# The product stage's first five h tiles: loaded by the up stage into the room of the up weights

## The chip, the cores and the metric

The kernel runs on one core of one Trainium2 chip. The metric is the device time of one execution in microseconds (us). The engines named here are PE (TensorE, matmuls), DVE (VectorE), ACT (ScalarE), POOL (GpSimd) and SP (SyncE, which in these stages issues every DMA).

## What is computed

The reference is a decoder layer on 4 sequences of 1024 tokens of width 512: self-attention with a norm, cross-attention with a norm, and a gated feed-forward of inner width 1536 in which the tensors are quantised and dequantised between the steps. The change concerns the feed-forward alone:

```python
def act_qdq(x):
    qmax = 2.0 ** (ACT_BITS - 1) - 1.0
    scale = jnp.maximum(jnp.max(jnp.abs(x)) / qmax, 1e-12)
    return jnp.clip(jnp.round(x / scale), -qmax - 1.0, qmax) * scale
...
x = act_qdq(x)
up = act_qdq(x @ lpbq_dequant(w_up).T)
gate = act_qdq(x @ lpbq_dequant(w_gate).T)
sig = fixed_qdq_u16(jax.nn.sigmoid(gate))
gate = act_qdq(gate * sig)
o = act_qdq(gate * up)
return o @ lpbq_dequant(w_down).T
```

Each `act_qdq` needs the largest magnitude of a whole tensor before its first element can be quantised. So the stages of the feed-forward can't flow into one another: each ends with a maximum, and the next begins with a scale.

## The kernel before, in words

All tensors of the feed-forward are feature-major: a tile has 128 features in the partitions and tokens along the free dimension. There are T = 4096 tokens, 8 groups of 512 tokens, and 12 feature tiles f of 128 features. Features 0 to 5 (RES = 6) of the up product stay in SBUF (`rows`, called `res` in the functions); features 6 to 11 ("spilled") are written to the HBM tensor `scr_up` (`y_dram`).

**The up stage** (`up_phase`, L1806) takes 96 steps n, of 512 tokens and one feature tile each. In a step PE makes twelve matmuls with the up weights `wu_hi` and `wu_lo`; SP loads a gate tile (`load_gate`, L1852), ACT, POOL and DVE make h = gate * sigmoid(gate) of it in a ring of seven buffers `v_w`, and SP stores it to the HBM tensor `scr_h` (`store_h`, L1858); for the spilled features SP stores an up tile too (L1872). SP's instructions are one queue in written order: behind step 95's up store stand `store_h(NT - 1)`, the store of the last h tile, and then waits until every store has landed:

```python
                store_h(NT - 1)
                for j in range(NY):
                    sp.wait_ge(y_out[j], 16 * sum(1 for m in range(NG * (FT - RES)) if m % NY == j))
                for j in range(NW):
                    sp.wait_ge(h_out[j], 16 * sum(1 for n in range(NT) if n % NW == j))
```

The block of the stage (L1839) ends in a barrier of all engines. Then the stage's semaphores are cleared (L59), and a second barrier follows (L60); `Kit.clear` does both, once for each kit that has semaphores.

**The quantisers** (`quantisers`, "quh") turn the two maxima into scales, with a few small instructions of DVE and PE and barriers of their own.

**The product stage** (`product_phase`, L1975) takes 48 tiles of 128 x 1024 in f32 (512 KB), features in the order 0, 6, 1, 7, 2, 8 and so on, four token blocks of each; so four tiles whose up part is in `rows` alternate with four spilled ones. Per tile ACT quantises h (L2045) and up (L2049), DVE multiplies (L2064) and takes the maximum of the tile before (L2057). SP loads h from `scr_h` into a ring of six buffers `j_h` (L2019), for spilled tiles also up from `scr_up` into `j_u` (L2024), and stores a spilled tile's result to `scr_o` (L2036). The load of tile n waits for the product of tile n - 6, and step n of SP's loop issues load n + 5 ahead of the store of tile n, which waits for product n. Before the loop SP issues the loads of tiles 0 to 4.

Then `product_quantiser` and `down_phase` follow; the latter is the second large matmul stage and ends the kernel.

Of the kernel before, what the change touches and what calls it, by code (L numbers as in the profile page):

```python
# [49 lines left out]
class Kit:  # L50


    def __init__(self, nc, ctx):
        self.nc, self.ctx, self.sems = nc, ctx, []
        ctx.callback(self.clear)
# [1747 lines left out]
                dve.wait_ge(scaled, 2)  # L1803


def up_phase(nc, x_dram, scale, wts, gate_dram, sg, isg, hunit, y_dram, res, h_dram, ymax, hmax):  # L1806

# [2 lines left out]
    with ExitStack() as ctx:  # L1812
# [26 lines left out]
        with nc.Block() as block:  # L1839

            @block.sync
            def _(sp):
                def load_x(g):
                    for j, dst in enumerate((xh, xl)):
                        sp.dma_start(dst[g % 2][:], x_dram[j][g]).then_inc(x_in[g % 2], 16)

                def load_gate(n):
                    g, o = divmod(n, FT)
                    if n >= NW:
                        sp.wait_ge(hmaxed, n - NW + 1)  # L1850
                        sp.wait_ge(h_out[n % NW], 16 * (n // NW))
                    sp.dma_start(wk[n % NW][:], gate_dram[o, :, g * GT:(g + 1) * GT]).then_inc(g_in[n % NW], 16)  # L1852

                def store_h(n):
                    g, o = divmod(n, FT)
                    sp.wait_ge(prod, n + 1)
                    sp.sem_inc(stood, 1)
                    sp.dma_start(h_dram[o, :, g * GT:(g + 1) * GT], wk[n % NW][:]).then_inc(h_out[n % NW], 16)  # L1858

                load_x(0)  # L1860
                for n in range(NW - LATE):
                    load_gate(n)
                load_x(1)
                for n in range(NT):
                    g, o = divmod(n, FT)
                    if n + NW - LATE < NT:
                        load_gate(n + NW - LATE)
                    if n > 0:
                        store_h(n - 1)
                    if o >= RES:  # L1870
                        sp.wait_ge(evicted, n + 1)
                        sp.dma_start(y_dram[o, :, g * GT:(g + 1) * GT], y[spilled(n) % NY][:]).then_inc(y_out[spilled(n) % NY], 16)  # L1872
                    if o == FT - 1 and g + 2 < NG:
                        sp.wait_ge(summed, n + 1)
                        load_x(g + 2)
                store_h(NT - 1)
                for j in range(NY):
                    sp.wait_ge(y_out[j], 16 * sum(1 for m in range(NG * (FT - RES)) if m % NY == j))
                for j in range(NW):
                    sp.wait_ge(h_out[j], 16 * sum(1 for n in range(NT) if n % NW == j))  # L1880
# [91 lines left out]
                dve.wait_ge(done, 2)  # L1972


def product_phase(nc, h_dram, y_dram, res, ish, isu, o_dram, omax):  # L1975

    W, NH, NU, NO = 1024, 6, 4, 4
    TR = T // W  # L1980
    rows, spare = list(range(RES)), list(range(RES, FT))
    order = []
    while rows or spare:
        order += [rows.pop(0)] if rows else []
        order += [spare.pop(0)] if spare else []
    tiles = [(f, j) for f in order for j in range(TR)]
    NT = len(tiles)
    with ExitStack() as ctx:
        kit = Kit(nc, ctx)
        h = [kit.sb(f"j_h{j}", [P, W], F32) for j in range(NH)]  # L1990
        u = [kit.sb(f"j_u{j}", [P, W], F32) for j in range(NU)]
        o = [kit.sb(f"j_o{j}", [P, W], F32) for j in range(NO)]
        magic = kit.sb("j_magic", [P, 1], F32)
        tmax = kit.sb("j_tmax", [P, NT], F32)
        h_in, u_in, stored = ([kit.sem(f"j_{n}{j}") for j in range(k)] for n, k in (("h_in", NH), ("u_in", NU), ("out", NO)))
        ready, added, prod, maxed, done, stood = (kit.sem(f"j_{n}") for n in ("ready", "added", "prod", "maxed", "done", "stood"))

        def spilled(n):
# [13 lines left out]
        with nc.Block() as block:  # L2012
            @block.sync
            def _(sp):
                def load(n):
                    f, j = tiles[n]
                    if n >= NH:
                        sp.wait_ge(prod, n - NH + 1)
                    sp.dma_start(h[n % NH][:], h_dram[f, :, j * W:(j + 1) * W]).then_inc(h_in[n % NH], 16)  # L2019
                    m = spilled(n)  # L2020
                    if m is not None:
                        if m >= NU:
                            sp.wait_ge(prod, tile_of(m - NU) + 1)
                        sp.dma_start(u[m % NU][:], y_dram[f, :, j * W:(j + 1) * W]).then_inc(u_in[m % NU], 16)  # L2024
# [201 lines left out]
def feed_forward(nc, c, res, moments, x1_dram, w_dram, scratch, out):  # L2226
# [4 lines left out]
    with ExitStack() as ctx:  # L2231
# [8 lines left out]
        with ExitStack() as up_scope:  # L2240
            wu = [Kit(nc, up_scope).sb(f"wu_{n}", [P, FT, KT, P], F16) for n in ("hi", "lo")]
            with ExitStack() as gate_scope:
# [7 lines left out]
                quantisers(nc, c, "qx", [of("x")])  # L2250
                gate_phase(nc, c, x2, res[:, T // P * D:], x2_dram, scale["x"], inverse["x"], wg, gate_dram, x_dram, pmax["gate"], tiles(wu, 1) + down_tiles)
            quantisers(nc, c, "qg", [of("gate")])
            up_phase(nc, x_dram, scale["x"], wu, gate_dram, scale["gate"], inverse["gate"], hunit, up_dram, res, h_dram,
                     pmax["up"], pmax["h"])
        quantisers(nc, c, "quh", [of("up"), of("h", hunit)])
        product_phase(nc, h_dram, up_dram, res, inverse["h"], inverse["up"], o_dram, pmax["o"])
        product_quantiser(nc, c, pmax["o"], scale["h"], scale["up"], scale["o"], inverse["o"])
        down_phase(nc, o_dram, res, scale["o"], inverse["o"], wd, x2_dram, out)

# [52 lines left out]
```

## Time and profile before

| what | value |
|---|---|
| time, median of 3 runs | 3060.09 us (3058.86 to 3063.71) |
| the profiled execution, its own time | 3056.02 us |
| its span in the trace | 3054.2 us |
| PE busy, share of the span | 86% |
| DVE, ACT, POOL busy | 74%, 61%, 59% |
| up stage | from 2390 us to 2652 us of the span |
| product stage | from 2656.7 us to 2781.8 us |
| down stage | from 2785 us to the end |

Positions in the trace are microseconds from the start of the span. A DMA has two times: SP issues it, which takes some 0.3 to 0.5 us of SP's queue, and it lands later; the landing raises the semaphore that others wait for. Rates in GB/s are what the 16 DMA engines moved together.

### The profile page before, as it was taken

How to read it: one execution, taken by the hardware profiler on the slowest of the kernel's cores; microseconds unless marked ns; L12 is line 12 of the kernel's file. 1: busy time of each engine (PE TensorE's matmuls, PEld its weight loads, DVE VectorE, ACT ScalarE, POOL GpSimd, SP SyncE). 2: the span in 40 equal slices, each digit the busy share in tenths (PEclk: the TensorE clock that was granted, in tenths of full speed). 3: DMA queues.
4: the chain of work that ended last, by engine and by line, in shares of the span. 5: the costliest groups of instructions: out<-in, count | busy, mean ns of one | idle time of the engine just before them, and what ended most of it. 6: DMA issues, size and time to landing. Idle time of an engine off the chain costs nothing. (4 is left out here: it accounts for less than half of the span.)

```text
span 3054.2 us, 77257 instructions
## 1 busy us (share of the span) xinstructions
PE 2622.1 (86%) x24103; PEld 1414.8 (46%) x24103; DVE 2263.1 (74%) x4431; ACT 1872.6 (61%) x3765; POOL 1815.2 (59%) x1209
## 2 busy tenths in 40 slices
PE   7999688888886969999999999993999899603999
PEld 4555345555554534555555555551444344201444
DVE  8888767777775777888888888865333477697776
ACT  3444377777775536777777777774333577695333
POOL 3444489999997317999999999994000244300000
PEclk9999889999998989999999999996999999856999
DMA  8999634434445661223233242235443688796332
GB/s 305 334 334 329 220 101 127 137 126 136 133 133 171 234 231 48 54 83 88 78 114 90 78 122 83 82 88 188 167 165 151 219 278 287 267 417 252 127 112 82
DMA packets 331176, 517.02 MB, mean 169 GB/s; under 512 B 41057, under 2 KB 162785, under 8 KB 331058
## 3 DMA queue, kind: packets, MB, share of 16 engines
q1 hardware_dynamic: 327586, 508.88, 50.1%
q0 software_dynamic: 1952, 6.29, 0.7%
q8 instruction: 55, 0.90, 0.1%
q10 hardware_dynamic: 1520, 0.43, 0.1%
q14 instruction: 63, 0.52, 0.0%
HBM read 266.10 MB, written 194.28 MB: 151 GB/s over the span
## 5 line engine op out<-in xcount | busy, mean ns | idle before, releaser
L1301 POOL TENSOR_TENSOR cross_plo<-cross_p 128x2048 f16<-128x2048 f32 (+1 forms) x256 | 856.7, 3376 | 46.1 <-ACT cross_p L1082 46.1
L1196 DVE CUSTOM_DVE_ANT_0 cross_junk<-cross_sc,rows 128x1024 bf16<-128x1024 f32 x512 | 617.9, 1222 | 109.1 <-PE cross_sc L946 101.4
L1082 ACT ACTIVATE cross_p<-cross_st 128x512 f32<-128x512 f32 x1024 | 556.1, 595 | 210.2 <-PE cross_st L993 210.1
L1301 POOL TENSOR_TENSOR self_plo<-self_p 128x1024 f16<-128x1024 f32 (+7 forms) x512 | 576.8, 1160 | 15.2 <-ACT self_p L1082 14.7
L1082 ACT ACTIVATE self_p<-self_st,self_strip 128x512 f32<-128x512 f32 (+3 forms) x768 | 414.7, 582 | 141.0 <-PE self_st L991 110.8
L1196 DVE CUSTOM_DVE_ANT_0 self_junk<-self_sc,self_strip 128x1024 bf16<-128x1024 f32 (+7 forms) x512 | 371.1, 753 | 133.4 <-PE self_sc L952 132.4
L988 PE MATMUL cross_st<-cross_qa,cross_ka 97*128 97x512 f16 x1024 | 395.7, 386 | 2.6 <-DMA cross_qa<-cross_mrow 1.2
L993 PE MATMUL cross_st<-rows,idbig 128*128 128x512 f16 x1024 | 391.3, 382 | 0.0
L1017 PEld LDWEIGHTS cross_o<-cross_vh,cross_p 128*128 128x128 bf16 x4096 | 270.9, 97 | 78.1 <-issue 24.5
L1017 PE MATMUL cross_o<-cross_vh,cross_p 128*128 128x65 f16 x4096 | 298.1, 191 | 7.0 <-POOL cross_plo L1301 6.8
L1928 POOL TENSOR_SCALAR v_w<-v_w 128x512 f32<-128x512 f32 x96 | 59.8, 623 | 400.1 <-ACT v_w L1905 400.0
L1018 PE MATMUL cross_o<-cross_vh,cross_plo 128*128 128x33 f16 x4096 | 291.7, 179 | 0.0
L988 PE MATMUL self_st<-self_qa,self_ka 98*128 98x512 f16 (+3 forms) x768 | 244.1, 333 | 50.8 <-ACT self_p L1082 46.0
L1018 PEld LDWEIGHTS cross_o<-cross_vh,cross_plo 128*128 128x128 f16 x4096 | 250.0, 96 | 53.4
L952 PE MATMUL self_sc<-self_ka,self_qa 96*128 96x512 f16 (+3 forms) x768 | 213.0, 334 | 33.7 <-DMA self_ka<-scr_k_hi 18.7
L1017 PE MATMUL self_o<-self_vh,self_p 128*128 128x65 f16 x2304 | 199.3, 192 | 40.1 <-DVE self_osum L1219 19.8
L130 PE MATMUL gt_acc<-rows,wg_hi 128*128 128x512 f16 x768 | 229.9, 381 | 1.5 <-DVE rows L124 1.5
L945 PE MATMUL cross_sc<-cross_ka,cross_qa 32*128 32x512 f16 x512 | 200.4, 392 | 21.2 <-DMA cross_kx<-scr_k_hi 12.3
L946 PE MATMUL cross_sc<-cross_kx,cross_qa 32*128 32x512 f16 x512 | 200.4, 392 | 0.0
L1017 PEld LDWEIGHTS self_o<-self_vh,self_p 128*128 128x128 bf16 x2304 | 163.2, 98 | 74.3 <-issue 43.1
L1018 PE MATMUL self_o<-self_vh,self_plo 128*128 128x33 f16 x2304 | 192.0, 179 | 0.0
L988 PEld LDWEIGHTS cross_st<-cross_qa,cross_ka 97*128 97x128 f16 x1024 | 99.7, 97 | 188.4 <-ACT cross_p L1082 94.8
(266 smaller groups left out, 5859.0 us busy)
## 6 DMA issues: line engine op xcount, KB each, us to landing
self_strip<-self_strips SPq DMA_DIRECT2D x64, 516.0 KB, 3.2
scr_gate<-gt_y SPq DMA_DIRECT2D x96, 256.0 KB, 2.1
v_w<-scr_gate SPq DMA_DIRECT2D x96, 256.0 KB, 4.0
scr_h<-v_w SPq DMA_DIRECT2D x96, 256.0 KB, 4.1
j_h<-scr_h SPq DMA_DIRECT2D x48, 512.0 KB, 9.5
d_o<-scr_o SPq DMA_DIRECT2D x9, 1536.0 KB
scr_up<-v_y SPq DMA_DIRECT2D x48, 256.0 KB, 4.2
j_u<-scr_up SPq DMA_DIRECT2D x24, 512.0 KB, 12.2
```

Source lines behind the costliest of these rows:

```text
L130: mm = nc.tensor.matmul(out, a, b, start=(n == 0), stop=(n == len(terms) - 1))
L945: nc.tensor.matmul(sc[slot % 2][:, 0:GT], qa[j][0:HD, qt * P:(qt + 1) * P], ka[j][0:HD, 0:GT], start=True, stop=True)
L946: nc.tensor.matmul(sc[slot % 2][:, GT:S], qa[j][HD:2 * HD, qt * P:(qt + 1) * P], kx[j][HD:2 * HD, :], start=True, stop=True).then_inc(scor ...
L952: mm = nc.tensor.matmul(sc[slot % 2][:, k - k0:k - k0 + w], qa[j][0:3 * HD, qt * P:(qt + 1) * P], ka[j][0:3 * HD, k:k + w], start=True, st ...
L988: mm = nc.tensor.matmul(out[:, 0:w], lhs, qa[j][0:KR, q0:q1], start=True, stop=causal)
L993: mm = nc.tensor.matmul(out[:, 0:w], c["idbig"][:], nm[kt][:, q0:q1], start=False, stop=True)
L1017: nc.tensor.matmul(out[:, qt % 4, :], high[:, q], vh[n % NQK][:, kt, :], start=first, stop=False, skip_group_check=True)
L1018: mm = nc.tensor.matmul(out[:, qt % 4, 0:HD + 1], rest[:, q], vh[n % NQK][:, kt, 0:HD + 1], start=False, stop=last_kt, skip_group_check=True)
L1082: nc.scalar.activation(p32[j][:, b + q0 - a:b + q1 - a], stp[cc % 2][:, 0:q1 - q0], ACT.Exp, bias=bias, scale=SM).then_inc(expd, 1)
L1196: nc.vector.tensor_tensor_reduce(junk[slot % 2][:, 0:w], sc[slot % 2][:, 0:w], bias, 1.0, -3e38, ALU.add, ALU.max, qmax[n % 2][:, qt:qt + ...
L1301: nc.gpsimd.tensor_tensor(plo[j][:, a:z], p32[j][:, a:z], high, ALU.subtract).then_inc(lo_g, 1)
L1928: nc.gpsimd.tensor_scalar(wk[n % NW][:], wk[n % NW][:], 65536.0, MAGIC, ALU.mult, ALU.add).then_inc(inc, 1)
```

## The change

The product stage's six h buffers are no longer tiles of their own: they become views into the up weights `wu_hi` and `wu_lo`, whose last reader is the last matmul of the up stage. A class `EarlyProducts` holds these views, their six semaphores and the first five tiles of the product's order, which are (feature, token block) = (0, 0), (0, 1), (0, 2), (0, 3) and (6, 0).

- In the up stage SP, after the up store of step 95 and before `store_h(NT - 1)`, waits for the last matmul (`summed` at NT), then for the stores of `scr_h` that the five tiles read, and issues the five loads.
- In the product stage SP issues no h load for tiles 0 to 4; the up load of tile 4 stays.
- The room of the up weights and the new semaphores live until the end of the product stage: the quantisers and the product stage move inside `up_scope`. When that scope ends, the kit of `EarlyProducts` clears its semaphores, with one more barrier of all engines, between the product stage and `product_quantiser`.

```diff
@@ up_phase, sync
                     if o == FT - 1 and g + 2 < NG:
                         sp.wait_ge(summed, n + 1)
                         load_x(g + 2)
+                sp.wait_ge(summed, NT)
+                for k, (f, j) in enumerate(following.tiles):
+                    n = ((j + 1) * (PW // GT) - 1) * FT + f
+                    sp.wait_ge(h_out[n % NW], 16 * (n // NW + 1))
+                    following.load(sp, k)
                 store_h(NT - 1)
@@ new
+PW, PH = 1024, 6
+class EarlyProducts:
+    def __init__(self, kit, wu, h_dram):
+        whole = [w[:].rearrange("p t k n -> p (t k n)").bitcast(F32) for w in wu]
+        each = FT * KT * P // 2 // PW
+        self.h = [whole[j // each][:, j % each * PW:(j % each + 1) * PW] for j in range(PH)]
+        self.h_in = [kit.sem(f"j_h_in{j}") for j in range(PH)]
+        self.h_dram, self.tiles = h_dram, product_order()[:PH - 1]
+
+    def load(self, sp, n):
+        f, j = self.tiles[n]
+        sp.dma_start(self.h[n], self.h_dram[f, :, j * PW:(j + 1) * PW]).then_inc(self.h_in[n], 16)
@@ product_phase
-        h = [kit.sb(f"j_h{j}", [P, W], F32) for j in range(NH)]
+        h, h_in = given.h, given.h_in
@@ product_phase, sync, load(n)
                     if n >= NH:
                         sp.wait_ge(prod, n - NH + 1)
-                    sp.dma_start(h[n % NH][:], h_dram[f, :, j * W:(j + 1) * W]).then_inc(h_in[n % NH], 16)
+                    if n >= NH - 1:
+                        sp.dma_start(h[n % NH][:], h_dram[f, :, j * W:(j + 1) * W]).then_inc(h_in[n % NH], 16)
@@ feed_forward
             quantisers(nc, c, "qg", [of("gate")])
+            given = EarlyProducts(Kit(nc, up_scope), wu, h_dram)
             up_phase(nc, x_dram, scale["x"], wu, gate_dram, scale["gate"], inverse["gate"], hunit, up_dram, res, h_dram,
-                     pmax["up"], pmax["h"])
-        quantisers(nc, c, "quh", [of("up"), of("h", hunit)])
-        product_phase(nc, h_dram, up_dram, res, inverse["h"], inverse["up"], o_dram, pmax["o"])
+                     pmax["up"], pmax["h"], given)
+            quantisers(nc, c, "quh", [of("up"), of("h", hunit)])
+            product_phase(nc, given, h_dram, up_dram, res, inverse["h"], inverse["up"], o_dram, pmax["o"])
         product_quantiser(nc, c, pmax["o"], scale["h"], scale["up"], scale["o"], inverse["o"])
```

## Rows read from the trace of the kernel before

**Rows 1.** Page: span; chain that ended last, by engine.

```profile
span 3054.2 us, 77257 instructions
PE 8%; DVE 0%; DMA 0%; ACT 0%; issue 0%; DVEq 0%; ACTq 0%
```

**Rows 2.** Windows by stage: length, each engine's busy time, clock, DMA share, GB/s.

```profile
2390.00:2651.90 261.90, 250.90 (x1152) 113.13 (x1152) 181.17 (x290) 193.78 (x289) 115.18 (x192) 0.98 0.83 273
2651.90:2656.70 4.80, 0.69 (x2) 0.32 (x2) 2.01 (x10) 0.00 (x0) 0.00 (x0) 0.50 0.00 0
2660.00:2776.00 116.00, 0.00 (x0) 0.00 (x0) 105.50 (x92) 110.35 (x95) 0.00 (x0) 0.50 1.03 416
```

**Rows 3.** Timeline, ACT, in the product stage: start, duration, idle before.

```profile
2709.45 1.24 ACT L2045 ACTIVATE j_h<-j_h,j_magic,inverse_h 128x1024 f32<-128x1024 f32 x1 [1.01 <-DMA j_h<-scr_h]
...
2769.79 1.24 ACT L2045 ACTIVATE j_h<-j_h,j_magic,inverse_h 128x1024 f32<-128x1024 f32 x1 [1.01 <-DMA j_h<-scr_h]
```

**Rows 4.** Lines, product stage: busy, mean ns of one.

```profile
L2045 ACT ACTIVATE j_h<-j_h,j_magic,inverse_h 128x1024 f32<-128x1024 f32 x48 | 59.1, 1231 | 19.1 <-DMA j_h<-scr_h 18.7
```

**Rows 5.** DMA view, product stage: packets, MB, share of 16 engines.

```profile
q1 hardware_dynamic: 13824, 50.34, 100.4%
```

**Rows 6.** Timeline, DVE, ACT and PE at the boundary of the two stages.

```profile
2644.99 0.38 PE L130 MATMUL v_acc<-v_xh,wu_lo 128*128 128x512 f16 x1
2650.69 0.23 DVE L1971 TENSOR_REDUCE pmax_h<-v_htmax 128x1 f32<-128x96 f32 x1
2652.75 0.23 DVE L1672 COPY quh_wide<-pmax_up 128x128 f32<-128x128 f32 x1 [1.83 <-PEq L60]
2656.78 0.06 DVE L2053 MEMSET j_magic<- 128x1 f32 x1 [1.34 <-PEq L60]
2660.75 1.24 ACT L2045 ACTIVATE j_h<-j_h,j_magic,inverse_h 128x1024 f32<-128x1024 f32 x1 [14.65 <-DMA j_h<-scr_h]
```

**Rows 7.** Timeline, SP's queue: start and duration of each DMA issue.

```profile
2648.09 0.42 SPq L1872 DMA_DIRECT2D scr_up<-v_y  x1
2649.51 0.32 SPq L1858 DMA_DIRECT2D scr_h<-v_w  x1
2656.70 2.34 SPq L2019 DMA_DIRECT2D j_h<-scr_h  x5
...
2664.40 0.32 SPq L2019 DMA_DIRECT2D j_h<-scr_h  x1
```

**Rows 8.** Waits of SP's queue, 2645 to 2662: us in total, times, longest.

```profile
SPq L1880 <- DMA scr_h<-v_w: 1.5, 1, 1.5
```

**Rows 9.** DMA issues, one each, tiles 0, 1, 2, 3, last h store: us to landing.

```profile
j_h<-scr_h SPq DMA_DIRECT2D x1, 512.0 KB, 4.0
...
j_h<-scr_h SPq DMA_DIRECT2D x1, 512.0 KB, 5.0
...
j_h<-scr_h SPq DMA_DIRECT2D x1, 512.0 KB, 5.8
...
j_h<-scr_h SPq DMA_DIRECT2D x1, 512.0 KB, 6.6
...
scr_h<-v_w SPq DMA_DIRECT2D x1, 256.0 KB, 2.0
```

**Rows 10.** DMA issues at 2556.6 to 2558, a gate tile behind two x loads.

```profile
v_xh<-scr_xq_hi SPq DMA_DIRECT2D x1, 512.0 KB, 6.4
...
v_w<-scr_gate SPq DMA_DIRECT2D x1, 256.0 KB, 7.8
```

**Rows 11.** Page, DMA issues of the gate tiles: median us to landing.

```profile
v_w<-scr_gate SPq DMA_DIRECT2D x96, 256.0 KB, 4.0
```

**Rows 12.** Line L2036, the product's stores: landing, shortest, median, longest.

```profile
DMA to landing us min/median/max: 2.6/8.7/9.9
```

**Rows 13.** Lines L1839 and L60 at 2652: barrier, clear, barrier.

```profile
L1839 DVEq EVENT_SEMAPHORE  x1: 21/21/21, 2652.0 to 2652.0; - x1
...
L60 DVEq EVENT_SEMAPHORE  x1: 21/21/21, 2652.6 to 2652.6; - x1
```

More of the change, by code:

```diff
@@ L1803, in _, with up_phase @@
                 dve.wait_ge(scaled, 2)
-def up_phase(nc, x_dram, scale, wts, gate_dram, sg, isg, hunit, y_dram, res, h_dram, ymax, hmax):
+def up_phase(nc, x_dram, scale, wts, gate_dram, sg, isg, hunit, y_dram, res, h_dram, ymax, hmax, following):
     NT, NR, NY, NW, LATE = NG * FT, 4, 3, 7, 3
@@ L1972, in _, with product_order @@
                 dve.wait_ge(done, 2)
-def product_phase(nc, h_dram, y_dram, res, ish, isu, o_dram, omax):
-    W, NH, NU, NO = 1024, 6, 4, 4
-    TR = T // W
+PW, PH = 1024, 6
+def product_order():
     rows, spare = list(range(RES)), list(range(RES, FT))
@@ L1985, in product_phase @@
         order += [spare.pop(0)] if spare else []
-    tiles = [(f, j) for f in order for j in range(TR)]
+    return [(f, j) for f in order for j in range(T // PW)]
+class EarlyProducts:
[8 more added lines that the diff above has]
+        sp.dma_start(self.h[n], self.h_dram[f, :, j * PW:(j + 1) * PW]).then_inc(self.h_in[n], 16)
+def product_phase(nc, given, h_dram, y_dram, res, ish, isu, o_dram, omax):
+    W, NH, NU, NO = PW, PH, 4, 4
+    TR = T // W
+    tiles = product_order()
     NT = len(tiles)
@@ L1994, in product_phase @@
         tmax = kit.sb("j_tmax", [P, NT], F32)
-        h_in, u_in, stored = ([kit.sem(f"j_{n}{j}") for j in range(k)] for n, k in (("h_in", NH), ("u_in", NU), ("out", NO)))
+        u_in, stored = ([kit.sem(f"j_{n}{j}") for j in range(k)] for n, k in (("u_in", NU), ("out", NO)))
         ready, added, prod, maxed, done, stood = (kit.sem(f"j_{n}") for n in ("ready", "added", "prod", "maxed", "done", "stood"))
```

## The prediction

> **What bounds the kernel now.** I read the page first. The chain that ended last names only 8% of the span [rows 1], all in the down stage, because it can't be followed back over the barriers that part the stages. So the change has to be judged from its own stretch, stage by stage: whatever moves the end of the product stage moves everything behind it by as much, and nothing before step 95 of the up stage is touched.
>
> The windows by stage come next [rows 2]. In the up stage PE is busy for 250.9 of 261.9 us. Between the stages, from 2651.9 to 2656.7, DMA moves nothing. In the product stage, from 2660 to 2776, DMA's share is 1.03 and it moves 416 GB/s without a break, while ACT has 110.35 us of work in 116. So DMA looks like the bound there. The timeline of ACT agrees: from tile 21 on it stands still for 1.01 us at every eighth tile until an h tile has landed, the first time before 2709.45 and the fourth before 2769.79, so 20.11 us apart [rows 3]. Up to the first stop it took 2709.45 - 1.01 - 2660.75 = 47.7 us for 21 tiles [rows 3, 6], 2.27 us each; eight tiles at that pace are 18.2 us; eight tiles of transfers are 8 h loads, 4 up loads and 4 stores of 512 KB, 8.39 MB, and at 416 GB/s these are 20.2 us. The stage as a whole moves 50.34 MB [rows 5], 96 transfers of 1.26 us. What is worth something in this stage is DMA work taken out of it, not a shorter wait of an engine.
>
> Then the boundary [rows 6, 7, 8]. PE's last matmul starts at 2644.99, DVE's last maximum at 2650.69. SP issues the last h store at 2649.51, and it lands 2.0 us later [rows 9], at 2651.5; SP is held for 1.5 us until then [rows 8], and it is the last to reach the barrier. The quantisers start at 2652.75, and the product stage's SP issues its first load at S = 2656.70, 5.2 us after that landing. ACT starts at 2660.75, 4.05 us after S, with tile 0.
>
> **The change, step by step.** *(a) The five loads in the up stage.* SP is through with the up store at 2648.51 [rows 7]. PE is long done, and the `scr_h` tiles that the five loads read were stored long before (the latest is step 84, eleven steps of 261.9 / 96 = 2.7 us back [rows 2]), so none of the new waits costs more than its own execution, some 0.03 us (a semaphore instruction of DVE is 21 ns [rows 13]). From 2648.55 SP issues five loads; the same five take 2.34 us in the product stage [rows 7]. With six waits SP arrives at the last h store at about 2651.06 instead of 2649.51, 1.55 us late by issue alone.
>
> The larger cost is what that store finds ahead of it. Nothing else queues on SP behind the loads but this store and the waits for all stores, and all engines wait for SP in the barrier. In the product stage the same five loads, issued from an empty queue, landed 4.0, 5.0, 5.8 and 6.6 us after their issues (tiles 0 to 3, issued 0.47 us apart) [rows 9]: tile 3 is there 8.0 us after the first issue, and tile 4, whose landing has no row, I put one transfer later, at 9.3. The store is a half transfer, 0.63 us: 9.9. So it lands at 2648.55 + 9.9 = 2658.4 instead of 2651.5, a delay of 6.9 us. That a small transfer is held by large ones ahead of it is seen twice: a product store takes 2.6 us alone and 9.9 in a full queue [rows 12], and the gate tile issued behind the two x loads took 7.8 us, where the median is 4.0 [rows 10, 11].
>
> Bounds of (a): below, the store overtakes the loads and costs only its late issue, 1.55 us. Above, each load ahead holds it as an x load held the gate tile, (7.8 - 4.0) / 2 = 1.9 us instead of 1.26, which adds 3.2: 10.1. I take 6.9, because the rows of the very same five loads are nearest.
>
> The Trainium skill, in "DMA: Bandwidth & Descriptors", section "Queues, rings and completion order", speaks against this change as well: the semaphore increment is a strongly ordered write, which lands only after every earlier write of the same DMA engine. By that rule the store's semaphore can't rise before the fifth load's data is written, and the sum keeps 6.9; without any holding it would have 1.55 in its place. The product's stores [rows 12] fit the rule; no row here shows a store right behind five loads.
>
> *(b) The product stage has five transfers fewer.* S moves with the barrier. DMA has 91 transfers to make from S on instead of 96: 5 x 1.26 = 6.3 us less, as long as DMA stays the bound and has work.
>
> *(c) Does DMA stay fed?* Before, eight transfers (five h, u, h, u) are issued at once, 10 us of work, and the next load comes with product 0 at 2664.40, 7.7 us after S [rows 7]. After, three transfers (u, h, u) are issued at once, 3.8 us of work. ACT no longer waits for tile 0 and can start at about S + 0.2, the time of the memset of `j_magic` [rows 6] and its semaphore; product 0 follows 3.65 us later (2660.75 to 2664.40), at S + 3.85, and one product each 2.27 us from there. A load lands 4.0 us after its issue, of which 1.26 is the transfer [rows 9], so its data flows after 2.7. Transfers are then done at S + 2.7 + 3.8 = 6.5, and the next two flow from S + 3.85 + 2.7 = 6.55: no gap. The pair for tile 7 keeps up; tiles 8 and 9 are rows tiles with one load each, and there the supply falls behind by about 0.5 us before the stores of tile 4 and on fill the queue again. I take 0.6 us; it is 0 if the queue's start is quicker once warm, and 1.9 if every load needs the full 4.0. ACT alone would be done with 45 tiles at S + 0.2 + 102, and DMA lets it have tile 45 at about S + 106 (before: 2769.79, S + 113): DMA is still the bound.
>
> *(d) The semaphores of EarlyProducts.* One more clear and barrier stand on the path after the product stage. At 2652 the release of one barrier to that of the next, with the clear between, is 0.6 us [rows 13]. POOL, which clears, has nothing else to do there. Below 0.5 or above 0.7 there is no reason.
>
> *(e) Nothing else.* The wait for `summed` is hidden by SP's own work. The h tiles' other place in SBUF changes no instruction's size: ACT and DVE work on the same shapes (L2045, 1231 ns [rows 4]). Six of the product kit's semaphores are cleared elsewhere.
>
> The sum is 6.9 - 6.3 + 0.6 + 0.6 = +1.8 us. The room in which DMA was idle, 5.2 us from the last store's landing to S plus the 2.7 before data flows, is still there: it only comes after the five loads instead of before them, since the barrier waits for the queue. On the profiled execution that makes 3056.02 + 1.8 = 3057.8; the median of the runs is 4.07 above that execution, and on it the forecast is 3061.9.
>
> **The rivals.** *A, the store is not held.* It lands at 2651.06 + 2.0 = 2653.1, and the loads run on under the barriers and the quantisers, as the change means them to. Then the sum is 1.55 - 6.3 + 0.6 + 0.6 = -3.5, time 3056.6. For it: DMA is idle from 2651.5 on, room enough. Against it: the held transfers [rows 10, 12]. The Trainium skill's rule to issue a DMA early and wait for it late, so that its fixed cost overlaps ("DMA: Bandwidth & Descriptors", "Rules for kernel authors"), would promise this side; here a store's landing is waited for right behind the loads [rows 8].
>
> *B, the other side: the burst runs at the rate of the x loads.* With 1.9 us for each of the five loads before the barrier, and 1.26 won back for each behind it, the sum is 1.8 + 3.2 = +5.0, time 3065.1. It is slower by over 0.2% from 2.1 us a load on (5 x 0.86 = 4.3 more than my sum). For it: the gate tile [rows 10]. Against it: those x loads had stores and gate tiles around them, and the same h loads took 1.26 in the product stage.
>
> *C, ACT's start decides.* If the product stage followed its first tile and not its transfers, it would begin 6.9 - (4.05 - 0.2) = 3.05 us later, and with (d) the sum is +3.65, time 3063.7. For it: before, ACT ran 21 tiles without a stop. Against it: the stops [rows 3], which only a backlog of DMA explains.
>
> **How the numbers follow.** Mine has 0.60, A 0.16, B 0.12, C 0.12. About 0.2% is what a measurement of this kernel tells from no change, 6.1 us. No case reaches it by its own sum; the runs before differ by 4.9 us among themselves, so I add 1.5 to 2 us on either side. The range reaches from A to between C and B with that scatter: 3055.5 to 3066.0. Within 0.2%: 0.90. Slower by more: B's upper half and the scatter, 0.07. Faster by more: A with luck, 0.03.
>
> **What would show it.** (a) The last `scr_h` store is issued at about 2651 and lands some 7 us later; SP's wait at L1880's place grows from 1.5 to about 7; the five early loads land between 2652.5 and 2658. Right for A would be a store that lands in 2 to 3 us. (b) The product's SP starts at about 2663.6, ACT 0.2 us later and without a wait for tile 0; the stops at every eighth tile stay, and the stage is about 6 us shorter, counted from its first issue. (c) A window of 1 us with less than 400 GB/s some 12 to 14 us into the stage. (d) Two pairs of clear and barrier before `product_quantiser`. The prediction is wrong if the store lands early, if the stops vanish, or if the stage isn't shorter by the five transfers.

## The result, and the profile after

The changed kernel takes 3065.59 us (median of 22 runs, 3058.98 to 3068.73), the kernel before 3059.34 us (22 runs, 3056.39 to 3063.71) in the same comparison. The ratio is 1.0019, 95% interval 1.0012 to 1.0025: slower by 5.8 us, between 3.7 and 7.7 (the two medians as they stand differ by 6.25). The forecast was 3061.9 us, +1.8 us, with a range of 3055.5 to 3066.0. The direction and the range held, the range by 0.4 us; the size is three times the forecast's sum.

**Where to measure.** The spans of the two profiled executions differ by 10.3 us (3054.2 and 3064.5), more than the runs do. The reason stands at the boundary of the stages. DVE's timeline, before the change for the end of the product stage, and after it for both ends (start, duration, idle before):

```profile
2780.92 0.20 DVE L2069 TENSOR_REDUCE pmax_o<-j_tmax 128x1 f32<-128x48 f32 x1
2782.38 0.23 DVE L2088 COPY qo_wide<-pmax_o 128x128 f32<-128x128 f32 x1 [1.26 <-PEq L60]
...
2785.45 0.06 DVE L2194 MEMSET d_magic<- 128x1 f32 x1 [1.21 <-DVEq L60]
```

```profile
2655.37 0.23 DVE L1976 TENSOR_REDUCE pmax_h<-v_htmax 128x1 f32<-128x96 f32 x1
2665.18 0.23 DVE L1672 COPY quh_wide<-pmax_up 128x128 f32<-128x128 f32 x1 [9.58 <-PEq L60]
...
2669.20 0.06 DVE L2083 MEMSET j_magic<- 128x1 f32 x1 [1.34 <-PEq L60]
...
2790.89 0.20 DVE L2099 TENSOR_REDUCE pmax_o<-j_tmax 128x1 f32<-128x48 f32 x1
2792.76 0.23 DVE L2118 COPY qo_wide<-pmax_o 128x128 f32<-128x128 f32 x1 [1.67 <-PEq L60]
...
2795.82 0.06 DVE L2224 MEMSET d_magic<- 128x1 f32 x1 [1.20 <-PEq L60]
```

DVE's last maximum of the up stage, `pmax_h`, starts at 2650.69 before [rows 6] and at 2655.37 after: 4.7 us later. No instruction of the other engines ahead of it was changed, and PE's last matmul already starts 5.7 us later (2650.69 against 2644.99 [rows 6]). Over all the profiled executions of this study `pmax_h` lies anywhere from 2650.6 to 2661.0. From there on the executions without early loads repeat one another to about 0.1 us (`pmax_h` to S is 6.01 to 6.05 us in five of them), so every comparison below is of the **stretch** from the start of `pmax_h` to the start of the memset of `d_magic`, which begins the down stage. It is 2785.45 - 2650.69 = 134.76 us before and 2795.82 - 2655.37 = 140.45 us after: **+5.69 us**, close to the 5.8 us of the runs. No kernel has a second profiled execution, and where the store is held or the stage starts slowly the scatter is larger than 0.1 us: the changed kernel and e13, the same up to S, have 13.75 and 14.34 us there. So differences below some 0.6 us between such kernels aren't read. The parts of the stretch, with S for SP's first issue in the product stage:

| part | before | after | difference | forecast |
|---|---|---|---|---|
| `pmax_h` to S (a) | 6.01 | 13.75 | +7.74 | +6.9 |
| S to `pmax_o` (b and c) | 124.22 | 121.77 | -2.45 | -5.7 |
| `pmax_o` to `qo_wide` (d) | 1.46 | 1.87 | +0.41 | +0.6 |
| `qo_wide` to `d_magic` | 3.07 | 3.06 | 0 | 0 |
| sum | 134.76 | 140.45 | +5.7 | +1.8 |

**The held store.** SP's queue after the change (compare [rows 7]), then SP's wait (compare [rows 8]), then the landings of early loads 1 to 4 and of the last h store, one issue each (compare [rows 9]):

```profile
2652.77 0.42 SPq L1872 DMA_DIRECT2D scr_up<-v_y  x1
2653.29 1.42 SPq L2006 DMA_DIRECT2D wu_hi<-scr_h  x3
2654.75 0.97 SPq L2006 DMA_DIRECT2D wu_lo<-scr_h  x2
2655.84 0.64 SPq L1858 DMA_DIRECT2D scr_h<-v_w  x1
2669.12 0.32 SPq L2054 DMA_DIRECT2D j_u<-scr_up  x1
```

```profile
SPq L1885 <- DMA scr_h<-v_w: 7.3, 1, 7.3
```

```profile
wu_hi<-scr_h SPq DMA_DIRECT2D x1, 512.0 KB, 4.9
...
wu_hi<-scr_h SPq DMA_DIRECT2D x1, 512.0 KB, 5.8
...
wu_hi<-scr_h SPq DMA_DIRECT2D x1, 512.0 KB, 6.5
...
wu_lo<-scr_h SPq DMA_DIRECT2D x1, 512.0 KB, 7.2
...
scr_h<-v_w SPq DMA_DIRECT2D x1, 256.0 KB, 8.1
```

The last h store is issued 0.47 us after `pmax_h` (before: 1.18 us ahead of it) and lands 8.1 us later instead of 2.0. SP waits 7.3 us for it where it waited 1.5, and every engine waits for SP. In the trace the five loads go by the room of the weights that they fill, `wu_hi` and `wu_lo`. The trace also has the packets of each queue, and the store's can be told by their size, 2 KB where the loads' have 4 KB: the loads' data flow from 2654.7 to 2662.9, the store's 128 packets only from 2662.0 to 2663.5, and it lands at 2663.9. So it is the store's own data that stand behind the loads' in the queue, and not only its semaphore that is late.

**The product stage.** ACT starts 0.17 us after S, without a wait for a tile, but the first stop for DMA comes at tile 13 already, 30.3 us after S, where it came at tile 21 [rows 3]. Later stops are at every eighth tile as before. ACT's timeline:

```profile
2669.29 1.24 ACT L2075 ACTIVATE wu_hi<-wu_hi,j_magic,inverse_h 128x1024 f32<-128x1024 f32 x1 [17.49 <-DVE j_magic L2083]
...
2699.43 1.24 ACT L2075 ACTIVATE wu_hi<-wu_hi,j_magic,inverse_h 128x1024 f32<-128x1024 f32 x1 [0.60 <-DMA wu_hi<-scr_h]
...
2719.53 1.24 ACT L2075 ACTIVATE wu_lo<-wu_lo,j_magic,inverse_h 128x1024 f32<-128x1024 f32 x1 [1.04 <-DMA wu_lo<-scr_h]
...
2779.79 1.24 ACT L2075 ACTIVATE wu_lo<-wu_lo,j_magic,inverse_h 128x1024 f32<-128x1024 f32 x1 [1.03 <-DMA wu_lo<-scr_h]
```

The windows show why (last two figures: DMA's share, GB/s). First the kernel before, from 4 us after S on, then the changed kernel, the first 4 us, the next 24, and the rest:

```profile
2660.70:2684.70 24.00, 0.00 (x0) 0.00 (x0) 20.51 (x19) 23.95 (x22) 0.00 (x0) 0.50 1.02 413
2684.70:2772.00 87.30, 0.00 (x0) 0.00 (x0) 81.54 (x72) 82.51 (x71) 0.00 (x0) 0.50 1.03 417
```

```profile
2669.12:2673.12 4.00, 0.00 (x0) 0.00 (x0) 1.28 (x2) 3.83 (x4) 0.00 (x0) 0.50 0.76 225
2673.12:2697.12 24.00, 0.00 (x0) 0.00 (x0) 23.16 (x21) 24.00 (x22) 0.00 (x0) 0.50 0.99 359
2697.12:2785.00 87.88, 0.00 (x0) 0.00 (x0) 80.44 (x71) 82.22 (x71) 0.00 (x0) 0.50 1.03 418
```

DMA moves 359 GB/s instead of 413 for 24 us and is at its old rate from then on. Counted in transfers of 512 KB, it has moved 18.2 of them 28 us after S instead of 20.7: 2.5 transfers, 3.1 us, of the five that were taken out of the stage are lost there. The share hardly shows it: 0.99 against 1.02.

The mix of loads and stores isn't the reason. SP issues no store in the first 12 us of the stage in either kernel, and in the windows from 4 to 8 and from 8 to 12 us after S DMA moves 419 and 402 GB/s before, 384 and 359 after.

### The profile page after: what moved, and what is told of

It reads as the page before. It is cut to its first block and busy times, and to the rows that moved or that the text cites. A ratio compares the mean times of both kernels' runs of the same rounds, so it can differ in the third digit from the quotient of the medians.

```text
span 3064.5 us, 77271 instructions
## 1 busy us (share of the span) xinstructions
PE 2629.2 (86%) x24103; PEld 1415.8 (46%) x24103; DVE 2264.6 (74%) x4431; ACT 1875.0 (61%) x3765; POOL 1815.1 (59%) x1209
## 5 line engine op out<-in xcount | busy, mean ns | idle before, releaser
L945 PE MATMUL cross_sc<-cross_ka,cross_qa 32*128 32x512 f16 x512 | 200.9, 393 | 20.7 <-DMA cross_kx<-scr_k_hi 11.8
## 6 DMA issues: line engine op xcount, KB each, us to landing
wu_lo<-scr_h SPq DMA_DIRECT2D x24, 512.0 KB, 10.7
```

The source lines that it names most:

```text
L945: nc.tensor.matmul(sc[slot % 2][:, 0:GT], qa[j][0:HD, qt * P:(qt + 1) * P], ka[j][0:HD, 0:GT], start=True, stop=True)
```

## The experiments

All stretches are from one profiled execution each; e7, e10, e12 and e13 ran only this once, so they have no ratio. S is SP's first issue in the product stage. "Moved" is what DMA has moved 28 us after S, in transfers of 512 KB, summed from windows of 4 us. In e1, e4, e8, e11 and e12, where early loads are still in flight at S, it holds up to 0.9 of a transfer of them: in e1 DMA moves 301 GB/s in the first 4 us and not 225, which is 0.6 of a transfer.

| kernel | `pmax_h` to S | stage, S to `pmax_o` | moved | stretch | against before |
|---|---|---|---|---|---|
| before | 6.01 | 124.22 | 20.7 | 134.76 | |
| changed | 13.75 | 121.77 | 18.2 | 140.45 | +5.69 |
| e1 store first | 7.03 | 121.16 | 19.0 | 133.13 | -1.63 |
| e2 none early | 6.02 | 124.18 | 20.7 | 135.14 | +0.38 |
| e3 two early | 9.80 | 122.30 | 20.2 | 137.04 | +2.28 |
| e4 store first, ring of 8 | 7.10 | 118.25 | 20.9 | 130.27 | -4.49 |
| e5 none early, ring of 8 | 6.01 | 124.17 | 20.5 | 135.09 | +0.33 |
| e7 none early, ring of 5 | 6.03 | 126.40 | 19.4 | 137.36 | +2.60 |
| e8 store first, six, ring of 8 | 7.74 | 117.41 | 21.2 | 129.64 | -5.12 |
| e9 loads from ACT's queue | 12.16 | 120.54 | 18.6 | 137.65 | +2.89 |
| e10 none early, one gap | 6.05 | 129.27 | 20.6 | 140.24 | +5.48 |
| e11 as e8, issue split | 6.42 | 118.41 | 21.7 | 129.32 | -5.44 |
| e12 store first, ring of 7 | 7.14 | 119.12 | 20.3 | 131.17 | -3.59 |
| e13 changed, ring of 8 | 14.34 | 117.67 | 20.5 | 136.93 | +2.17 |

**e1: the store first.** The edit swaps the two steps:

```diff
+                store_h(NT - 1)
                 sp.wait_ge(summed, NT)
                 for k, (f, j) in enumerate(following.tiles):
                     ...
                     following.load(sp, k)
-                store_h(NT - 1)
```

> The change with one swap: the last h store is issued ahead of the five early loads. Measured on the stretch from the start of the up maximum's reduce (pmax_up/pmax_h pair, pmax_h) to the memset of d_magic: 134.8 us before, 140.5 after. Theory H (the barrier waits for the store, and the store waits for the loads): SP is free for the barrier some 0.9 us later than before (its five issues), so the first issue of the product stage comes 6.9 us after pmax_h instead of 6.0 (before) and 13.75 (after); stage as in the changed kernel, 121.8 us from that issue to pmax_o; stretch about 133.8 us, time 1 us below before. Rival (DMA's increments wait for everything issued in the meantime, or the barrier waits for the loads themselves): the swap gains nothing, stretch about 140.

S comes 7.03 us after `pmax_h` instead of 13.75, so 6.7 of the 7.7 us at the boundary were the store's place behind the loads. SP's queue shows that the rest is the time of its five issues:

```profile
2652.43 0.32 SPq L1858 DMA_DIRECT2D scr_h<-v_w  x1
2652.84 1.35 SPq L2006 DMA_DIRECT2D wu_hi<-scr_h  x3
2654.24 1.05 SPq L2006 DMA_DIRECT2D wu_lo<-scr_h  x2
2660.64 0.32 SPq L2054 DMA_DIRECT2D j_u<-scr_up  x1
```

`pmax_h` is at 2653.61 here; SP is through at 2655.3, 1.7 us behind it, where it was 0.9 behind in the kernel before, and the store has landed by then: no wait for a DMA is left in SP's queue. The barrier doesn't wait for the loads. Time: 3056.62 us against 3059.30, ratio 0.9991 (0.9982 to 1.0000).

**e2: none early.** Only the room in the weights and the extra kit stay:

```diff
-        self.h_dram, self.tiles = h_dram, product_order()[:PH - 1]
+        self.h_dram, self.tiles = h_dram, product_order()[:0]
...
-                    if n >= NH - 1:
+                    if n >= 0:
```

> The changed kernel without any early load: h tiles still in the room of the up weights, semaphores in their own kit, all h loads issued at the product stage's start. Theory (only the extra clear and barrier are left, 0.4 us in the changed kernel's trace): stage from its first issue to pmax_o 124.2 us as before, stretch 134.8 + 0.4 = 135.2 us. Rival (the place of the h tiles in SBUF slows the stage, and that is why it was 2.45 us shorter and not 5.7): stage 125.5 to 127.5 us, stretch 136.5 to 138.5.

The stage takes 124.18 us (before 124.22), the stretch 135.14: the place of the h tiles costs nothing, the extra clear and barrier 0.4 us. Time: ratio 1.0009 (0.9999 to 1.0018).

**e3: two early,** still ahead of the store (`[:2]` and `n >= 2` in the same two places).

> The changed kernel with two early loads instead of five, still ahead of the last h store. Theory H: the store is held by 2 x 1.26 us plus about 1.2 us for the late issue and the start of the queue, so the product stage's first issue is some 3.7 us later than before, measured from pmax_h (9.7 us). The queue is not run dry at the start (six transfers are issued at once), so the stage is shorter by the full two transfers, 2.5 us (121.7), and the stretch is 134.8 + 3.7 - 2.5 + 0.4 = 136.4 us. Rival (the shortfall of the gain has nothing to do with a dry queue and is proportional to the tiles brought early): stage shorter by 1.0 us, stretch 137.9.

SP waits 5.1 us for the store:

```profile
SPq L1885 <- DMA scr_h<-v_w: 5.1, 1, 5.1
```

S comes 9.80 us after `pmax_h`: +3.8 for two loads, +7.7 for five, so 1.3 us for each load, one transfer, and 1.15 us once (with e13's 14.34 it is 1.5 for each load). The stage is 1.9 us shorter of the 2.5 that two transfers make, with 0.4 of a transfer lost by 28 us. The stretch is 0.6 longer than my 136.4, nearer to it than to the rival's 137.9, and the shortfall is not proportional: 0.2 of a transfer lost for each of two, 0.5 for each of five. Time: ratio 1.0005 (0.9995 to 1.0014).

**e4: the store first, and a ring of eight.** On top of e1's swap (left out are the lines for eight semaphores and for the same five early tiles):

```diff
-    W, NH, NU, NO = PW, PH, 4, 4
+    W, NH, NU, NO = PW, 8, 4, 4
...
-        h, h_in = given.h, given.h_in
+        h = given.h + [kit.sb(f"j_h{j}", [P, W], F32)[:] for j in range(PH, NH)]
```

> The store first, five early loads, and a ring of eight h buffers (six in the weights' room, two of their own) instead of six, so that the product stage issues h tiles 5, 6, 7 and up tiles 0 to 3 at once, seven transfers instead of three. Theory (the stage lost its gain because the queue ran dry in the first 28 us, 2.5 transfers short): the stage is shorter by the full five transfers, 124.2 - 6.3 = 117.9 us from its first issue to pmax_o; stretch 134.8 + 0.9 - 6.3 + 0.4 = 129.8, time 5 us below before. Rival (ACT or another limit holds the stage at 121.8): stretch 133.8.

With seven transfers issued at S instead of three, the slow stretch is all but gone. The same 24 us, from 4 us after S, in e1 and then in e4:

```profile
2664.64:2688.64 24.00, 0.00 (x0) 0.00 (x0) 23.16 (x21) 24.00 (x22) 0.00 (x0) 0.50 0.99 366
```

```profile
2672.13:2696.13 24.00, 0.00 (x0) 0.00 (x0) 23.16 (x21) 24.00 (x22) 0.00 (x0) 0.50 1.02 404
```

ACT and DVE do the same work in both. The stage takes 118.25 us, 6.0 shorter than before, near the full 6.3 of five transfers. The stretch is 0.5 longer than expected. Time: 3055.39 us against 3059.30, ratio 0.9985 (0.9975 to 0.9995).

**e5: a ring of eight alone,** none early.

> The changed kernel without early loads, with a ring of eight h buffers. Theory (with all loads issued at the product stage's start the queue is deep enough with six buffers already, and DMA is the bound): as the kernel with no early load, stage 124.2 us from its first issue to pmax_o, stretch 135.1 us. Rival (the deeper ring by itself gives what the store-first kernel with eight buffers gained, early loads or not): stretch 130 to 133.

124.17 and 135.09 us: by itself the deeper ring gives nothing. DMA is the bound of the stage, and only transfers taken out of it shorten it. Time: ratio 1.0005 (0.9996 to 1.0014).

**e7: a ring of five,** none early.

> The changed kernel without early loads, with a ring of five h buffers instead of six, so that fewer transfers stand in the queue at any time. Theory D (DMA's rate depends on how many transfers are queued: with two to five of them it moved some 350 GB/s at a share near 1 in the changed kernel, with more 417): the rate falls below 400 GB/s in the steady part of the stage with DMA's share still near 1, and the stage takes 128 us or more. Rival (the rate of a busy queue is 417 GB/s whatever its depth, and the loss came from moments in which nothing was queued): either 417 GB/s as before, or a share clearly below 1 in proportion to the lost rate.

This refutes theory D in its general form. In the steady part the rate is the old one, with landings down to 8.4 us from 10.7. Window and DMA view of e7:

```profile
2680.00:2760.00 80.00, 0.00 (x0) 0.00 (x0) 74.94 (x65) 77.18 (x65) 0.00 (x0) 0.50 1.03 417
```

```profile
wu_hi<-scr_h SPq DMA_DIRECT2D x15, 512.0 KB, 8.4
```

What e7 loses it loses at the start: 1.3 transfers within 28 us, when 6 were issued at S and none more for 5.4 us. The stage is 2.2 us longer. The loss belongs to the start of the stage, with few transfers queued, and not to a small ring as such. The number issued at S isn't the whole measure either: e3 issues six as well and loses 0.4 of a transfer, but two of its tiles have landed by then and ACT starts at once, so that its next load is issued 3.8 us after S and not 7.8.

**e8: six early behind the store, ring of eight, no extra barrier** (the semaphores of the ring go into the kit of the identities, which is cleared at the end of the kernel anyway). Shown is this line alone; the rest is as in e4, with six early tiles.

```diff
-            given = EarlyProducts(Kit(nc, up_scope), wu, h_dram)
+            given = EarlyProducts(c["kit"], wu, h_dram)
```

> Everything that the theory calls good together: the last h store first, six early loads, a ring of eight, and the semaphores of the h tiles in the kit of the identities, so that no extra clear and barrier follows the product stage. Expected against the store-first kernel with ring eight and five loads (stretch 130.27): one transfer more before the stage, -1.26, its issue on SP ahead of the barrier, +0.45, the barrier -0.41: stretch 129.1 us, time some 5.5 us below before. Rival (with six loads the last landings come after the product stage's start, so the sixth brings nothing): 130.3.

`pmax_o` to `qo_wide` is back at 1.42 us. The stretch is 129.64, 0.6 better than e4 where 1.2 was expected: SP's six issues end 2.4 us after `pmax_h` and move S to 7.74. Time: 3055.94 us against 3059.46, ratio 0.9987 (0.9978 to 0.9996).

**e9: the loads from ACT's queue.** ACT issues the five loads behind its last eviction; SP's queue is as before the change.

```diff
                     evict(n)
+                act.wait_ge(summed, NT)
+                for k, (f, j) in enumerate(following.tiles):
+                    n = ((j + 1) * (PW // GT) - 1) * FT + f
+                    act.wait_ge(h_out[n % NW], 16 * (n // NW + 1))
+                    following.load(act, k)
```

> The changed kernel with the five early loads issued by ACT behind its last eviction instead of by SP; SP's queue is as before the change. ACT is free some 4.6 us ahead of pmax_h. Theory H1 (the store was held because it stood behind the loads in the same queue): from ACT's queue the loads share the DMA engines with the last stores but don't stand ahead of them all; the last h store lands 3 to 5 us after its issue, the product stage's first issue comes 7 to 9 us after pmax_h. Theory H2 (a store's increment waits for every write issued earlier on the same DMA engines, whatever the queue): the five loads were issued 5 us before the store and hold it until they have landed, some 3 to 4 us after pmax_h: first issue 8.5 to 10 us after pmax_h. Rival N (loads in another queue cost the store nothing): 6.0 us. Stage from first issue to pmax_o 121.8 us in each case.

None of the three had the size: 12.16 us. Another queue doesn't spare the stores, it makes more of them late. ACT's two issues, then the landings of an up store issued at 2648.4 and of the last h store, issued at 2651.96:

```profile
2647.24 1.37 ACTq L2006 DMA_DIRECT2D wu_hi<-scr_h  x3
2648.66 1.31 ACTq L2006 DMA_DIRECT2D wu_lo<-scr_h  x2
```

```profile
scr_up<-v_y SPq DMA_DIRECT2D x1, 256.0 KB, 8.1
...
scr_h<-v_w SPq DMA_DIRECT2D x1, 256.0 KB, 8.1
```

The last h store lands at 2660.1, and no packet moves after 2659.8, though the loads were issued 2 to 5 us ahead of it and in another queue. N, that such loads cost nothing, is refuted, and so are the times of H1 and H2 (H2's end of the loads, 3 to 4 us after `pmax_h`, is 5.5 here). Which mechanism it is the packets of the two queues tell, which this trace keeps apart. SP issues five stores from 2648.0 to 2652.0, and not one of their packets moves before 2652.3, while the loads' do. From then on both queues move packets side by side, until the loads' data end at 2658.6. The last store's own 128 packets come from 2658.7 to 2659.8, and it lands 0.3 us later. So it is the sharing of the engines, H1's mechanism, that makes the store late, at more than H1's price; increments that wait for earlier writes ("DMA: Bandwidth & Descriptors" in the Trainium skill, "Queues, rings and completion order"), H2's mechanism, had nothing left to hold here. Why SP's stores stood still until 2652.3 is open. The stage, 120.54 us, is 1.2 shorter than in the changed kernel, with the same three transfers issued at S, so two slow starts can differ by that much. Time: ratio 1.0012 (1.0003 to 1.0021).

**e10: one gap in the middle.**

```diff
                 for n in range(NT):
+                    if n == 20:
+                        sp.wait_ge(prod, 24)
                     if n + NH - 1 < NT:
```

> The changed kernel without early loads, and one wait put into SP's queue in the middle of the product stage: at tile 20 no load is issued until product 23 is done, so that the queue of transfers runs short once (about 9 us without a new issue), 50 us into the stage. Theory R (a queue that has run short starts a stretch of some 20 us in which DMA moves only some 350 GB/s at a share near 1, even when landing times show that the queue is long again; this is what cost the changed kernel 2.5 transfers): after the gap, windows of 4 us at 340 to 380 GB/s for some 20 us, and 1 to 2 transfers lost beyond those of the gap itself. Rival (the slow stretch belongs to the start of the stage, not to a short queue): 416 GB/s in the first or second window after the gap.

Windows of 2 us around the gap:

```profile
2717.30:2719.30 2.00, 0.00 (x0) 0.00 (x0) 1.80 (x3) 1.96 (x3) 0.00 (x0) 0.50 0.40 158
2719.30:2721.30 2.00, 0.00 (x0) 0.00 (x0) 2.00 (x2) 2.00 (x2) 0.00 (x0) 0.50 0.00 0
2721.30:2723.30 2.00, 0.00 (x0) 0.00 (x0) 2.00 (x3) 0.18 (x1) 0.00 (x0) 0.50 0.91 209
2723.30:2725.30 2.00, 0.00 (x0) 0.00 (x0) 0.56 (x1) 0.13 (x1) 0.00 (x0) 0.50 1.01 385
2725.30:2727.30 2.00, 0.00 (x0) 0.00 (x0) 0.00 (x0) 2.00 (x2) 0.00 (x0) 0.50 0.99 373
2727.30:2729.30 2.00, 0.00 (x0) 0.00 (x0) 1.73 (x2) 1.91 (x3) 0.00 (x0) 0.50 1.04 424
```

Theory R falls: DMA is back at 424 GB/s 6 us after the first window with data. The stage is 5.1 us longer than in e2, and the first three windows alone lack 3.4 transfers against 417 GB/s, 4.2 us. A queue that runs dry once, and is then refilled in a burst (fourteen transfers in 9 us here), costs the gap and little more, no slow stretch of 20 us. It isn't a copy of the changed kernel's start, in which three transfers are issued and each next one waits for a product.

**e11: e8 with the issue split.** Two loads behind the store, four in the quantisers' block:

```diff
-                for k, (f, j) in enumerate(following.tiles):
+                for k, (f, j) in enumerate(following.tiles[:2]):
...
+            if given is not None:
+                @block.sync
+                def _(sp):
+                    for k in range(2, PH):
+                        given.load(sp, k)
```

> As the kernel with the store first, six early loads, ring of eight and shared kit, but only two of the six loads are issued in the up stage, behind the last h store, while SP waits for its landing anyway; the other four are issued by SP in the quantisers' block, in which it has nothing else to do. Expected: the first issue of the product stage is back at 6.0 us after pmax_h (7.7 with all six in the up stage); stage 117.4 us from there, a little more because the last of the six now flow into its first microseconds; stretch 128 to 129 us, time 6 us below before. Rival (four loads in flight in the quantisers' block slow its small instructions or the barriers): first issue at 7 us or later.

S is at 6.42, 1.3 us earlier than in e8; the stage gives 1.0 of it back, since the sixth load flows into its start. S was expected at 6.0, the rival had 7 or later. The stretch, 129.32, is the shortest of all, but by only 0.3 us from e8, which is too little for one execution each, and it is 0.3 above what was expected. Time: 3055.13 us against 3059.80, ratio 0.9986 (0.9977 to 0.9995). No interval parts e4, e8 and e11 from one another; all three lie below 1, which makes them faster than the kernel before by 4 to 5 us (the intervals reach from 1 to 8).

**e12 and e13: the dose, and whether the two losses add.** e12 is e1 with a ring of seven; e13 is the changed kernel, store last, with a ring of eight.

> The store first, five early loads, and a ring of seven h buffers: five transfers issued at the product stage's start instead of three (ring six) or seven (ring eight). Theory Q (what counts is how many transfers stand in the queue when ACT starts to use them up): between the two, some 0.6 of a transfer lost in the first 28 us (1.6 with three, none with seven), stage 119.5 to 120 us from its first issue, stretch 131.5 to 132. Rival (the second fresh buffer, or the phase of the ring against the order of the tiles, made the difference): 121 or 118 us.

> The changed kernel as it is, with its loads ahead of the last h store, but with a ring of eight h buffers. Theory (the two losses are separate and add: the held store 7.7 us at the boundary, the short queue about 3.5 us in the stage): first issue 13.7 us after pmax_h as in the changed kernel, stage 118.2 us as with ring eight, stretch 140.45 - 3.5 = 136.9 us. Rival (the loss in the stage comes with the late store or the landed loads, not with the queue): stage 121.8, stretch 140.5.

e12 lies between, as theory Q says, with the stage and the stretch 0.4 and 0.3 us below what was expected: three, five and seven transfers issued at S (e1, e12, e4) leave 19.0, 20.3 and 20.9 moved by 28 us (18.5, 19.9 and 20.2 without the early loads still in flight, from the first 4 us at 301, 272 and 316 GB/s) and stages of 121.16, 119.12 and 118.25 us. e13's stretch is 136.93 us where 136.9 was expected. So the held store and the weak start are separate and add up. Its two parts are each about 0.6 us off what was expected (14.34 and 117.67), in opposite directions.

## Why the prediction was right, and where it was off

*What bounds the stage* was read rightly: e5 shows that room alone brings nothing, e4 and e13 that transfers taken out do, at 1.2 and 1.3 us each.

*(a) The held store* is shown. The swap (e1) takes 6.7 of 7.7 us away, and the dose (e3) gives 1.3 us a load. The size, 6.9, was 0.8 short. The store's own landing took 8.1 us where the forecast had 2658.4 - 2651.06 = 7.3, and its issue was 1.65 us late in place of 1.55. Most of the 0.8 is the burst's own pace: the fourth load landed 2654.75 + 7.2 - 2653.29 = 8.7 us after the first was issued, where the rows gave 8.0.

*(b) and (c) The gain in the stage* is the step that was mis-sized. (b) itself, 6.3 us, holds where the queue is full (6.0 in e4, 6.5 in e13). (c) stood at 0.6 with an upper bound of 1.9, and it measured 3.85: 121.77 - (124.22 - 6.3). I asked only when the queue would be empty and counted a queue with anything in it as one that moves 417 GB/s. The rows show 359 GB/s for 24 us at a share of 0.99. One of the prediction's own signs of being wrong came true with it: the stage is 2.45 us shorter and not about 6, and instead of one weak window 12 to 14 us in there are 24 weak microseconds. So the sign of the mechanism was right, a stage that starts with three transfers instead of eight is worse fed, but the measure that I used for it, idle time, doesn't see most of it. The 2.5 transfers lost are 3.1 of the 3.85 us. The remainder of 0.7 is open: in the other kernels "moved" and the stage's length agree within some 0.6 us (e1, without its early loads, lost 2.2 transfers, 2.8 us, and its stage is 3.2 above the full gain).

*(d) The barrier* was 0.41 us in place of 0.6, below the 0.5 under which the prediction saw no reason for it (e2: 0.38 in the stretch; gone in e8).

*(e) Nothing else*: shown by e2, the same stage with the tiles in the weights' room.

*How much of the hit is luck.* The time, 3065.6, lies in the range because the range was stretched towards B and by scatter: the sum with its own upper bound of (c), 1.9, gives only +3.1 us, 3063.2. That the held store is dearer than the gain was foreseen, for the right reason; that it came out at +5.8 wasn't.

*The rivals.* A (the store is not held) is refuted by the wait of 7.3 us; e1 is what A would have looked like, and at -1.6 us it isn't -3.5 either, because (c) takes its part. B named the x loads' pace for the burst; the burst cost 1.3 us a load. But the time landed near B's 3065.1, for another reason than B's. C (ACT's start decides) had +3.65; the stops at every eighth tile speak against it, and so does e4, in which ACT starts as in e1 and the stage is 2.9 us shorter.

**What stays open** is why DMA moves only some 350 GB/s for so long. DMA's view of 12 us, first after the change (2685.12 to 2697.12, that is 16 to 28 us after S), then before it (2672.70 to 2684.70):

```profile
DMA packets 1154, 4.21 MB, mean 351 GB/s; under 512 B 128, under 2 KB 128, under 8 KB 1152
...
q1 hardware_dynamic: 1152, 4.19, 99.3%
...
j_u<-scr_up SPq DMA_DIRECT2D x4, 512.0 KB, 11.5
```

```profile
DMA packets 1361, 4.97 MB, mean 414 GB/s; under 512 B 148, under 2 KB 148, under 8 KB 1360
...
q1 hardware_dynamic: 1360, 4.96, 102.4%
...
j_u<-scr_up SPq DMA_DIRECT2D x3, 512.0 KB, 10.3
```

The engines are as busy (99.3% against 102.4%), and a packet takes longer in the mean, 16 x 12 us x 0.993 / 1152 = 0.166 us instead of 0.145. But this mean, over the 4 KB packets and the small ones, misleads. In the trace's own list of packets the median of a 4 KB packet is 159 ns in both windows. After the change 82 of 1026 take over 250 ns, up to 1.5 us, and hold 20% of the packets' time; before it is 7 of 1213 and 1.4%. So most packets run at the old pace and some stall. From 4 to 28 us after S the share of such packets is 6.7% in the changed kernel, 5.3% in e1 and 4.6% in e9 (three transfers at S), 3.2% in e7, 2.9% in e12, 2.2% in e4, 0.7% before and 0.4% in e11; later it is below 0.1% in all of these. What stalls them isn't shown.

By then transfers take 11.5 us to land, so they are not few any more. A short start brings the state on in a graded way (e1, e12, e4), a smaller ring in the steady state doesn't (e7), and neither does one dry queue that is refilled in a burst (e10).

## What to carry to other kernels

- A transfer that a barrier waits for must be issued ahead of those that it doesn't wait for. Here one swap of two lines made +5.7 us into -1.6; putting the loads into another engine's queue won back only half (e9, +2.9). When a load is moved to an earlier place, look first at what is queued behind it.
- Where DMA bounds a stage, prefetching into it pays only what it takes off the stage's own transfers, and only while the queue behind stays long: take the freed depth and issue more at the start (a ring of eight in place of six was worth 3 us more, and nothing without the early loads).
- Fix an anchor next to the change before comparing two profiles. The spans differed by 10.3 us and the stretch by 5.7, the runs by 5.8. The stretch also shows which part changed, which ratios of some ten runs with intervals of about 0.2% don't; how far it scatters has to be known for the part in question (0.1 us in an undisturbed boundary here, 0.6 where the store is held).

## What the runs showed of the hardware that was not expected

- DMA's share of busy time is no measure of its rate: 0.99 stood beside 359 GB/s and 1.02 beside 413, with 4 stores among the transfers issued in both windows. A packet that stalls counts as busy: 6.7% of the 4 KB packets took over 250 ns in the first case and 0.7% in the second, with a median of 159 ns in both.
- A store in SP's queue, issued 2 to 5 us behind five loads of ACT's queue, landed only when all queued transfers had been moved, 8.1 us after its issue (e9); with no loads about, it takes 2.0 us in the kernel before. Its data came last, not only its semaphore.
- A place in SBUF that matmul weights had left was as good as any other for tiles that DMA writes and ACT and DVE read (e2: 124.18 against 124.22 us).
